# Hybrid layer on one core: a new opening and new instruction orders, and residual sums of the second feed-forward and the channel mix moved from adding DMAs to VectorE

## The reference

```
n  = layernorm(x)
x += (n Wq^T n^T) n                     # linear attention; computed as n (Wq'(n^T n))
y  = layernorm(x);  z = y + relu(y W1 + b1) W2 + b2;  x += layernorm(z) * gamma + beta
n  = layernorm(x);  u = n + Wo(sigmoid(r) * wkv(k, v))   # k, v, r from LN1(n) and its shift by a token
                    # wkv is a recurrence along the tokens, with a running maximum
c  = LN2(u);        x += u + sigmoid(Wr c') * (relu(Wk c')^2 Wv)     # channel mix
y  = layernorm(x);  z = y + relu(y W1 + b1) W2 + b2;  x += layernorm(z) * gamma + beta
```

## Time and profile before

| | us |
|---|---|
| median of 3 runs | 283.79 |
| lowest, highest | 283.71, 286.62 |
| profiled execution, its own time | 286.06 |
| its span | 284.3 |
| mean granted clock of TensorE over the span | 0.981 |

### The profile page before, as it was taken

The page is one execution under the profiler, slowest core; times in us unless marked ns, Lnnn a source line. Parts: engine busy times, 40 slices in busy tenths (PEclk is TensorE's granted clock), DMA queues, the critical chain, the costliest instruction groups (busy, mean ns, idle before and its releaser), DMA issues. The chain is left out here.

```text
span 284.3 us, 5322 instructions
## 1 busy us (share of the span) xinstructions
PE 263.8 (93%) x1556; PEld 196.6 (69%) x1556; DVE 227.1 (80%) x739; ACT 229.8 (81%) x443; POOL 148.5 (52%) x294
## 2 busy tenths in 40 slices
PE   7598999997996999999999999999999989999990
PEld 7598688566684577477665676866757848777770
DVE  1648616889999999999999999999998499754224
ACT  2486994966598989997999998998999998788630
POOL 3474934654192599285882661953922524851331
PEclk9959999999999999999999999999999999999997
DMA  6910340220124122244404303225351405643132
GB/s 185 310 53 0 56 81 15 40 37 13 24 39 75 26 51 37 39 76 74 74 1 77 74 16 60 37 47 105 55 108 26 75 0 110 115 98 78 25 61 74
DMA packets 17740, 18.10 MB, mean 64 GB/s; under 512 B 1456, under 2 KB 11568, under 8 KB 17712
## 3 DMA queue, kind: packets, MB, share of 16 engines
q0 software_dynamic: 6480, 11.80, 24.3%
q1 hardware_dynamic: 11232, 5.97, 7.4%
HBM read 3.87 MB, written 2.10 MB: 21 GB/s over the span
## 5 line engine op out<-in xcount | busy, mean ns | idle before, releaser
L961 PEld LDWEIGHTS bank<-W,f_h 128*128 128x128 f32 x512 | 61.3, 192 | 9.9 <-issue 9.2
L961 PE MATMUL bank<-W,f_h 128*128 128x128 f32 x512 | 63.1, 275 | 0.3 <-ACT f_h L738 0.3
L945 PE MATMUL bank<-f_yT,W 128*128 128x512 f32 x128 | 62.6, 599 | 0.1
L738 ACT ACTIVATE f_h<-bank,B1C 128x512 f32<-128x512 f32 x64 | 42.5, 684 | 9.5 <-PE bank L945 9.3
L1003 PE MATMUL bank<-XK,FWk 128*128 128x512 f32 x64 | 32.2, 607 | 2.8 <-DVE XK L559 1.4
L945 PEld LDWEIGHTS bank<-f_yT,W 128*128 128x128 f32 x128 | 21.7, 190 | 18.3 <-issue 12.3
L1009 PEld LDWEIGHTS bank<-FWv,KK 128*128 128x128 f32 x256 | 30.5, 192 | 4.8 <-issue 2.2
L1009 PE MATMUL bank<-FWv,KK 128*128 128x128 f32 x256 | 31.2, 276 | 0.2 <-ACT KK L799 0.2
L394 DVE BATCH_NORM_STATS2 f_zn_stats<-bank 128x6 f32<-128x128 f32 x64 | 14.1, 282 | 18.3 <-PE bank L961 18.2
L678 ACT ACTIVATE f_y<-R,f_yn_nb,f_yn_rs 128x128 f32<-128x128 f32 x64 | 26.3, 485 | 2.6 <-POOL f_yn_nb L297 2.3
L440 DVE SCALAR_TENSOR_TENSOR f_zg<-bank,f_zn_rs,GAMMA 128x128 f32<-128x128 f32 x64 | 17.9, 341 | 7.6 <-issue 5.6
(11 more groups left out here) (133 smaller groups left out, 619.2 us busy)
## 6 DMA issues: line engine op xcount, KB each, us to landing
R<-BETA POOLq DMA_DIRECT2D x16, 256.0 KB, 3.5
R<-f_zg POOLq DMA_DIRECT2D x14, 256.0 KB, 3.4
R<-in_hidden SPq DMA_DIRECT2D x8, 256.0 KB, 4.7
R<-N POOLq DMA_DIRECT2D x8, 256.0 KB, 3.3
out_x<-R SPq DMA_DIRECT2D x8, 256.0 KB, 2.3
R<-G POOLq DMA_DIRECT2D x7, 256.0 KB, 3.4
W<-in_w SPq DMA_DIRECT2D x2, 256.0 KB, 4.5
BETA<-in_beta SPq DMA_DIRECT2D x1, 256.0 KB, 5.2
```

The costliest lines, as they stand in the source:

```text
L738: a.activation(at(f.h, b)[:, n, :], banks[bank][:], ACT.Relu, bias=B1C[:, n:n + 1]).then_inc(f.h_ready[n], 1)
L945: t_.matmul(banks[bank][:], W1[:, n * P:(n + 1) * P], at(f.yT, b)[:], start=True, stop=True).then_inc(f.h_psum[n], 1)
L961: last = t_.matmul(banks[bank][:, j * C:(j + 1) * C], at(f.h, b)[:, n, j * P:(j + 1) * P], W2[:, n, :], start=False, stop=(n == H - 1), sk ...
```

## The change

Six things are changed together.

- In the second feed-forward, batches 0 to 6 no longer call `ffn_start`. The bank holds h W2 alone. y is kept in SBUF; POOL's `down_residual` adds the centred b2 (as 4 x 128 columns, `B2R`) to it by an adding DMA, VectorE's `z_sum` adds the bank to it, `z_sum_stats` and `z_sum_scaled` work on it in place, and `ffn_add` adds it to `R[b]`. No `ffn_sum` is left there. `B2R` is made once, by `bias_diagonal`, `down_bias_part` and `down_bias_rows`.
- All batches of the channel mix end in `cmix_out` on VectorE; `cmix_sum` is gone.
- Batch 0 of the first and batch 7 of the second feed-forward are split in `ffn_gain` (bank times gamma) and `ffn_out` (times the scale, plus R).
- `attn_normed(0)` is made by VectorE; attention of batch 0 goes through to its end before the others; two more warm-up transposes; `centre_bias` comes later.
- y has four copies and h two in both feed-forwards. Some semaphores that counted all batches are split in two by parity. x0 of batch 3 is loaded before B1 and W1.
- The lists of calls of POOL, VectorE, ScalarE and TensorE are all new.

```diff
-COPIES = {"N": 3, "f1_y": 2, "f2_y": 2, "f1_yT": 2, "f2_yT": 2, "XN": 3, "XNT": 2, "GRAM": 2, "PROJ": 2, "f1_zg": 3, "f2_zg": 3, "others": 1}
-ADDED = {"f1": (0,), "f2": (7,), "x3": (7,)}
+COPIES = {"N": 3, "f1_y": 4, "f2_y": 4, "f1_yT": 2, "f2_yT": 2, "f1_h": 2, "f2_h": 2, "XN": 3, "XNT": 2, "GRAM": 2,
+          "PROJ": 2, "f1_zg": 3, "f2_zg": 3, "others": 1}
+ADDED = {"f1": (0,), "f2": tuple(range(BATCHES)), "x3": tuple(range(BATCHES))}
+SPLIT = {"f1": (0,), "f2": (7,)}
+IN_SBUF = {"f2": (0, 1, 2, 3, 4, 5, 6)}
...
-                self.scale = Steps(n + "_scale_steps", 1, *steps)
+                self.scale = Steps(n + "_scale_steps", 2, *steps)
...
             load_x0(2)
+            load_x0(3)
             sp.dma_start(B1[:], b1).then_inc(w1_loaded, DMA)
             sp.dma_start(W1[:], w1).then_inc(w1_loaded, DMA)
-            load_x0(3)
...
+            def down_residual(b, f):
+                if b == f.in_sbuf[0]:
+                    pool.wait_ge(b2_rows, 1)
+                pool.wait_ge(f.yT_psum, b + 1)
+                for earlier in f.yb.before(b):
+                    pool.wait_ge(*earlier)
+                pool.dma_start(at(f.y, b)[:], B2R[:], accum_op=ALU.add).then_inc(*f.yb.step(b))
...
-            def cmix_sum(b):
-                pool.wait_ge(*cgate.done(b, "kvs"))
-                pool.wait_ge(*x2u.ready(b))
-                if b >= 2:
-                    pool.wait_ge(*x3.ready(b - 2))
-                pool.dma_start(R[b][:], at(G2, b)[:].rearrange("p (j c) -> p j c", j=J), accum_op=ALU.add).then_inc(*x3.step(b))
...
+            def z_sum(b, f, bank):
+                dve.wait_ge(f.z_psum, b + 1)
+                dve.wait_ge(*f.yb.ready(b))
+                v.tensor_tensor(at(f.y, b)[:], bank_rows(bank), at(f.y, b)[:], ALU.add).then_inc(f.z_ready, 1)
+
+            def z_sum_stats(b, f):
+                dve.wait_ge(f.z_ready, f.in_sbuf.index(b) + 1)
+                row_stats(b, f.znorm, at(f.y, b))
...
+            def ffn_gain(b, f, bank):
...
+                v.tensor_tensor(at(f.zg, b)[:], bank_rows(bank), GAMMA[:].unsqueeze(1).broadcast_to([P, J, C]), ALU.mult).then_inc(f.zg_ready, 1)
+
+            def ffn_out(b, f):
+                dve.wait_ge(*f.znorm.scale.done(b, "rs"))
+                dve.wait_ge(f.zg_ready, b + 1)
+                dve.wait_ge(*f.xb.ready(b))
+                for j in range(J):
+                    last = v.scalar_tensor_tensor(R[b][:, j, :], at(f.zg, b)[:, j, :], f.znorm.rs[b % 2][:, j:j + 1], R[b][:, j, :],
+                                                  ALU.mult, ALU.add)
+                last.then_inc(*f.out.step(b))
...
+            def z_sum_scaled(b, f):
...
+                for j in range(J):
+                    last = v.scalar_tensor_tensor(y[:, j, :], y[:, j, :], f.znorm.rs[b % 2][:, j:j + 1], GAMMA[:], ALU.mult, ALU.mult)
                 last.then_inc(f.zg_ready, 1)
...
+            def attn_normed(b):
+                dve.wait_ge(na.mv_ready, b + 1)
+                dve.wait_ge(*na.scale.done(b, "rs"))
+                dst = at(XN, b)
+                for j in range(J):
+                    done = v.tensor_scalar(dst[:, j, :], R[b][:, j, :], na.mv[b % 2][:, j, 0:1], na.rs[b % 2][:, j:j + 1], ALU.subtract, ALU.mult)
...
```

The opening and the end of the new lists. POOL:

```diff
+            shift(0, na); power(0, na); shift(1, na); power(1, na); bias(0, na); shift(2, na); bias(1, na)
+            power(2, na); bias(2, na); shift(0, f1.norm); power(0, f1.norm); bias(0, f1.norm); shift(3, na)
...
+            ffn_residual(3, f2); z_shift(2, f2); power(2, f2.znorm); down_residual(5, f2); z_shift(3, f2)
+            ffn_residual(4, f2); tmix_residual(7); power(3, f2.znorm); shift(6, f2.norm); power(6, f2.norm)
+            bias(6, f2.norm); down_residual(6, f2); ffn_residual(5, f2); z_shift(4, f2); shift(7, f2.norm)
+            power(7, f2.norm); bias(7, f2.norm); power(4, f2.znorm); z_shift(5, f2); power(5, f2.znorm)
+            ffn_residual(6, f2); z_shift(6, f2); ffn_residual(7, f2); power(6, f2.znorm); z_shift(7, f2)
+            power(7, f2.znorm)
```

VectorE:

```diff
+            attn_stats(0); mean_var(0, na); attn_stats(1); mean_var(1, na); attn_normed(0); attn_stats(2)
+            mean_var(2, na); attn_stats(3); attn_out(0, 0); ffn_stats(0, f1); mean_var(0, f1.norm); centre_down_bias()
+            centre_down_weights(); attn_stats(4); mean_var(3, na); attn_out(1, 3); ffn_stats(1, f1)
...
+            z_sum_scaled(1, f2); ffn_add(1, f2, f2.y); tmix_out(7, 4); cmix_stats(7); mean_var(7, ncm)
+            z_sum(2, f2, 1); z_sum(3, f2, 6); z_sum_stats(2, f2); cgate_log(6, 5); mean_var(2, f2.znorm)
+            z_sum_stats(3, f2); mean_var(3, f2.znorm); z_sum_scaled(2, f2); cmix_change(7); cmix_k(7); cmix_r(7)
...
+            z_sum_scaled(6, f2); ffn_add(6, f2, f2.y); z_stats(7, f2, 2); mean_var(7, f2.znorm); ffn_gain(7, f2, 2)
+            ffn_out(7, f2)
```

ScalarE and TensorE:

```diff
+            gram_evacuate(0, 0); attn_evacuate(0, 1); proj_evacuate(0, 0); attn_normed(1); attn_normed(2)
+            attn_evacuate(1, 1); gram_evacuate(1, 2); attn_evacuate(2, 0); gram_evacuate(2, 3); proj_evacuate(1, 2)
+            ffn_normed(0, f1); proj_evacuate(2, 2); ffn_evacuate(0, f1, 0); attn_normed(3); relu(0, f1, 1, 1)
...
+            warm_up(0, 44); attn_gram(0, 0); attn_transpose(0, 1); attn_proj(0, 0); attn_apply(0, 0)
+            attn_transpose(1, 1); centre_bias(); attn_gram(1, 2); attn_transpose(2, 0, x1.ready(0)); attn_gram(2, 3)
+            attn_proj(1, 2); bias_part(); attn_proj(2, 2, (proj_ready, 2)); attn_apply(1, 3); ffn_transpose(0, f1, 0)
+            attn_apply(2, 2); hidden_up(0, f1, 2, 0); ffn_start(0, f1, 3, x1.ready(1)); hidden_up(0, f1, 1, 1)
...
+            product_o(7, 4); ffn_down(4, f2, 0, 7); ffn_down(4, f2, 1, 7); hidden_up(4, f2, 3, 3)
...
+            ffn_down(7, f2, 0, 2); ffn_down(7, f2, 1, 2); ffn_down(7, f2, 2, 2); ffn_down(7, f2, 3, 2)
```

More of the change, by code:

```diff
@@ L51, in hybrid_layer, with __init__ @@
         class Rows:
-            def __init__(self, name, added=()):
+            def __init__(self, name, added=(), moved=None):
                 self.added = tuple(added)
+                self.moved = [b for b in (range(B) if moved is None else moved) if b not in self.added]
                 self.sem_added = sem(name + "_added") if self.added else None
-                self.sems = [sem(f"{name}{n}") for n in range(2)] if len(self.added) < B else []
+                self.sems = [sem(f"{name}{n}") for n in range(2)] if self.moved else []
             def step(self, b):
@@ L64, in ready, with before @@
                     return self.sem_added, self.added.index(b) + 1
-                return self.sems[b % 2], DMA * len([c for c in range(b % 2, b + 1, 2) if c not in self.added])
+                return self.sems[b % 2], DMA * len([c for c in self.moved if c <= b and c % 2 == b % 2])
+            def before(self, b):
+                same = [c for c in self.moved if c < b and c % 2 == b % 2]
+                return [self.ready(same[-1])] if same else []
         def copies(name, shape, count):
@@ L131, in __init__ @@
                     self.nb = copies(n + "_nb", [P, J], 2)
-                    self.ready = Steps(dst_name + "_ready", 1, "but last", "all")
+                    self.ready = Steps(dst_name + "_ready", len(dst) if n == "attn" else 1, "but last", "all")
         class Ffn:
-            def __init__(self, n, stage, x):
-                self.stage = stage
+            def __init__(self, n, x):
                 self.x = x
@@ L236, in _ @@
             sp.dma_start(Wo[:], wo).then_inc(tmix_loaded, DMA)
-            for b in range(5, B):
-                load_x0(b)
+            load_x0(5)
+            load_x0(6)
+            load_x0(7)
             sp.dma_start(FWk[:], f_wk).then_inc(cmix_loaded, DMA)
@@ L326, in ffn_sum @@
                 pool.wait_ge(*f.xb.ready(b))
[L327 to L328 removed]
+                for earlier in f.out.before(b):
+                    pool.wait_ge(*earlier)
                 pool.dma_start(R[b][:], at(tile, b)[:], accum_op=ALU.add).then_inc(*f.out.step(b))
[L331 to L337 removed]
             def tmix_residual(b):
@@ L428, in attn_out @@
                 v.tensor_tensor(R[b][:], bank_rows(bank), R[b][:], ALU.add).then_inc(*x1.step(b))
+            def ffn_gain(b, f, bank):
+                if b == 0:
+                    dve.wait_ge(gamma_loaded, 2 * DMA)
+                dve.wait_ge(f.z_psum, b + 1)
+                if b >= len(f.zg) and b - len(f.zg) not in f.in_sbuf:
+                    dve.wait_ge(*f.out.ready(b - len(f.zg)))
+                v.tensor_tensor(at(f.zg, b)[:], bank_rows(bank), GAMMA[:].unsqueeze(1).broadcast_to([P, J, C]), ALU.mult).then_inc(f.zg_ready, 1)
[7 more added lines that the diff above has]
+                last.then_inc(*f.out.step(b))
             def ffn_scaled(b, f, bank):
@@ L435, in ffn_scaled @@
                 dve.wait_ge(*f.znorm.scale.done(b, "rs"))
-                if b >= len(f.zg):
+                if b >= len(f.zg) and b - len(f.zg) not in f.in_sbuf:
```

(7 more changed lines are left out.)

523 lines of the change are left out of this document (264 added, 259 removed).

## The result

The changed kernel takes **268.41 us** (median of four runs, 268.05 to 268.84) against 283.78; the ratio is 0.944, 95% interval 0.939 to 0.949. The forecast was 277.5, its range began at 271. The profiled execution took 268.56 us with a span of 266.7. Runs of the kernel before scatter from 282.1 to 287.5 us and those of the changed kernel by 0.8 us only, so other kernels are compared with the changed one by their own times, and with the kernel before by the ratio.

A forecast was written before the change was run, and what follows sets the result against it. TensorE and VectorE are both full from 60 to 242.5 us. TensorE's sum 240.4 + 27.5 + 6.7 = 274.6 and VectorE's 256.7 + 22.8 = 279.5 gave a span of 278.0, 6.3 less than now: 277.5 us, range 271 to 287.

The forecast's parts named there:

- The opening, step by step: Start of kernel: first attention sum at 13.0 us, first up-projection 19.7 instead of 32.3, z statistics at 29; 5.9 us less lost.
- The tail: After the last product: batch 7's gain is formed beside POOL's power, so 6.7 us instead of 7.4.
- The scaling's source at nothing: Second feed-forward's scaling reading SBUF instead of PSUM: no difference taken, bounds -1.7 us and +1 us.
- the later 12.8 as now: VectorE between first z statistics and tmix_out(7): 12.8 us of idle time carried over unchanged from the old order.
- the sum by VectorE: Span counted from VectorE's work and idle time: 256.7 plus 22.8 us idle, hence 279.5 us.
- By TensorE: Span counted from TensorE: 240.4 us of products, 27.5 lost to waits, 6.7 tail, 274.6 us.
- rival 1: TensorE's bound holds and its later waits shrink too: 269 to 273.5 us, chance 0.18.
- Identity adds: Seven ffn_start of the second feed-forward go: 7 x 0.44 = 3.1 us off TensorE, on the path.
- More is gained: The 15.6 us of later TensorE waits shrink as sums and buffers come free earlier: 269 to 273.5 us, chance 0.18.
- Start given back: Relus on ScalarE delay batch 0's downs; 5 to 7 us idle moves behind 42 us: 281 to 286.6 us, chance 0.17.
- VectorE the bound: From 60 us to tmix_out(7) VectorE bounds and idle stays 34.4 us: time 290.6 us, chance 0.11.
- POOL blocked: VectorE instructions with two SBUF inputs block POOL's chains, up to 1.1 us each, 12 us in all: 289.5 us, chance 0.04.

The follow-up runs named there:

- new_warm98: The changed kernel with 98 warm-up transposes instead of 44, so the first product starts later: 274.76 us.
- new_both_dma_early: The changed kernel with channel-mix and second feed-forward sums of batches 0 to 6 by adding DMAs, channel-mix DMAs called when data are ready, some statistics later: 275.22 us.
- new_identity: The changed kernel with the seven ffn_start back, z_sum a copy of the bank and down_residual out: 269.45 us.
- new_thin_sums: The changed kernel with its three vector sums done on one column of each 128, the rest left out: 267.62 us.

## Why the prediction missed

**What held.** The opening, step by step, within 1 us, and its passage to the end, shown for a later start (new_warm98). The tail. The count of TensorE's products, where it can be checked: 40.0 us from `product_o(7)` on, 39.6 measured without idle time. The scaling's source at nothing, and copies at nothing in the old order. VectorE's small price per sum (0.68 us).

**The step that failed** is "the later 12.8 as now": idle time of VectorE after the first z statistics, and with it TensorE's losses after the first up-projection (15.6 us), carried over from the old order. In the sum by VectorE the span came out 12.8 us under 279.5:

- Idle after the first z statistics and before `tmix_out(7)`: 4.5 us (2.6 up to 60 us, 1.9 behind), not 12.8. Before the z statistics it was 10.8, 10 forecast. Together **7.5 us**.
- Work before `tmix_out(7)`: 206.6 us, not 210.2. Busy time rose by 11.0 us in all, 15.7 were forecast. I added full durations, and instructions of VectorE overlap at their ends in the records: count times mean duration, over all groups, rises by 14.9 us (279.6 to 294.5), the busy time by 11.0. **3.6 us**, and it is no part of the real cause, since thinning VectorE's load by 10.5 us gave 0.8.
- Products from `product_o(7)` on, and tail: 39.6 and 6.5 us, not 41 and 6.7: **1.6 us**.

By TensorE: the last product ends at 260.2, L is 260.2 - 240.4 = 19.8 us, not 27.5. Up to the first up-projection 11.1 (11.9 forecast), behind it 8.7 instead of 15.6. I took a number between two bounds, 274.6 and 279.5; the lower one was itself 8 us too high, and so was rival 1, which starts from it.

**Why the later losses went.** Not by the engine of the sums into `R[b]`: with both by DMA (new_both_dma_early) the last `tmix_out` starts at 221.0, 0.9 us before the change. That kernel has the new opening and the new order and is 3.6% faster than before (some 10 us), where the change is 5.6%. The forecast had 5.9 us for the opening and nothing for the rest of the order. The sums on VectorE are worth the other 4 to 7 us, at the end of the kernel, where the chain gated product, sum, statistics of batches 5 and 6 has few products beside it. I had put no gain for that chain into either bound ("savings in the chain of x3 and the buffers are in neither"). Which of the moved calls removed the waits from 60 to 100 us, where TensorE had 4.7 us idle before (three waits, for a relu, for XK and for PROJ) and 0.04 after, stays open: no run takes the lists apart there. Two rivals are left beside the order, since every kernel with the new order has them: `z_sum` empties the bank of z into SBUF before its statistics (also in new_identity, as a copy), and h and y have more copies.

**Identity adds**: 3.1 us forecast, 1.0 measured by new_identity. The step "it is full in the middle, so this lies on the path" is wrong for four of the seven: they cost nothing before `tmix_out(7)`. The three behind it cost what was forecast. `down_residual` is gone in that kernel too, but nothing waits for it in the change.

**Rivals.** *More is gained* was the true side: the later waits shrank. It allowed up to 5 us of the 15.6 us of later waits to go; 6.9 went, and 268.4 lies below its 269. Its reason was that sums and buffers come free earlier. For the sums it holds only behind the last `tmix_out`; for the buffers no run of the new order tests it. *Start given back*, *VectorE the bound*: both refuted. TensorE has no idle time from 18.9 to 42 us, VectorE's idle time before `tmix_out(7)` fell to 15.3 us, and thinning its work gives 0.8 us. *POOL blocked*: neither its price nor its mark appeared. The mark was POOL's mean for four-column steps up by half. Over all of them (232 instructions) it is 539 ns before and 574 after, and without the power steps 334 and 333. Single groups moved both ways: `f_yn_ve` from 256 to 460 ns, `cmix_ve` from 593 to 441, as these lines of before and after show.

```profile
L269 POOL TENSOR_TENSOR cmix_ve<-cmix_mv,K_EPS 128x4 f32<-128x4 f32 x8 | 4.7, 593 | 1.0 <-DVE cmix_mv L422 1.0
...
L269 POOL TENSOR_TENSOR f_yn_ve<-f_yn_mv,K_EPS 128x4 f32<-128x4 f32 x16 | 4.1, 256 | 21.6 <-DVE f_yn_mv L422 21.6
```

```profile
L315 POOL TENSOR_TENSOR f_yn_nb<-f_yn_nm,f_yn_rs 128x4 f32<-128x4 f32 x16 | 7.9, 493 | 0.9
L284 POOL TENSOR_TENSOR f_yn_ve<-f_yn_mv,K_EPS 128x4 f32<-128x4 f32 x16 | 7.4, 460 | 37.5 <-DVE f_yn_mv L451 37.5
...
L284 POOL TENSOR_TENSOR cmix_ve<-cmix_mv,K_EPS 128x4 f32<-128x4 f32 x8 | 3.5, 441 | 6.4 <-DVE cmix_mv L451 6.4
```

In new_thin_sums:

```profile
L315 POOL TENSOR_TENSOR f_yn_nb<-f_yn_nm,f_yn_rs 128x4 f32<-128x4 f32 x16 | 8.5, 530 | 0.9
L284 POOL TENSOR_TENSOR f_yn_ve<-f_yn_mv,K_EPS 128x4 f32<-128x4 f32 x16 | 7.0, 440 | 33.6 <-DVE f_yn_mv L451 33.6
```

`f_yn_ve` stays at 440 ns when the sums are thinned: the added sums don't make its length. Which instructions do, no run here tells. POOL idles 43% of the span, so nothing waits long for it (4.6 us of ScalarE in all for `f_yn_nb`). VectorE's 15 sums of two SBUF tensors took 655 to 693 ns each. The Trainium skill, page "SBUF — State Buffer", section "SBUF: two separate sides", calls the port pair an exclusive lock on which whoever comes second waits. The long single steps of POOL would fit that, but the one test here, thinning the added sums, doesn't bear it out; a wait of VectorE for it shows in no row here.

**The range.** It gave 0.18 to this side and ended at 271, and both bounds shared the carried-over waits. An error common to both bounds isn't covered by the space between them.
